# Layer 1's experts over fifteen sorted tiles of 128 tokens

## The reference

```
def _moe(x, Wg, W1, b1, W2, b2):          # 1024 tokens, E = 8, D = 128, DF = 512
    xf = x.reshape(S * B, D)
    idx = jnp.argmax(xf @ Wg.T, axis=-1)
    out = jnp.zeros_like(xf)
    for e in range(E):
        m = (idx == e)[:, None].astype(xf.dtype)
        h = jax.nn.relu(xf @ W1[e] + b1[e])
        out = out + m * (h @ W2[e] + b2[e])
    return out.reshape(S, B, D)
y = _layer_norm(x + _mha(...), g1, be1)
z = _layer_norm(y + _moe(y, Wg, W1, b1, W2, b2), g2, be2)
```

## Time and profile before

| what | us |
|---|---|
| median of 3 runs | 1155.62 |
| lowest and highest of them | 1153.92, 1157.77 |
| span of the profiled execution | 1150.6 |
| its time outside the span | not listed; the median lies 5.0 above the span |
| TensorE busy (matmuls) | 949.3 (83%) |
| VectorE busy | 581.6 (51%) |
| ScalarE busy | 439.1 (38%) |
| GpSimd busy | 223.4 (19%) |

### The profile page before, as it was taken

The page is one execution under the profiler, slowest core; times in us unless marked ns, Lnnn a source line. Parts: engine busy times, 40 slices in busy tenths (PEclk is TensorE's granted clock), DMA queues, the critical chain, the costliest instruction groups (busy, mean ns, idle before and its releaser), DMA issues. The chain is left out here.

```text
span 1150.6 us, 15643 instructions
## 1 busy us (share of the span) xinstructions
PE 949.3 (83%) x5673; PEld 649.8 (56%) x5673; DVE 581.6 (51%) x1264; ACT 439.1 (38%) x769; POOL 223.4 (19%) x258
## 2 busy tenths in 40 slices
PE   6885799759947459999777968998699988879998
PEld 4673345349935236777537832233366676747776
DVE  4885446265377553111765857775264448631111
ACT  2341445433323013334352414776332233333443
POOL 0552301000053030000373534001000013320110
PEclk9995979869969759999997976999899989978999
DMA  7004410215410000110000051400001010000111
GB/s 305 1 33 106 127 31 23 111 73 160 138 33 0 1 0 19 38 37 19 1 1 1 2 133 36 116 22 2 0 29 41 27 38 1 1 1 19 37 37 37
DMA packets 30159, 52.72 MB, mean 46 GB/s; under 512 B 3152, under 2 KB 22800, under 8 KB 29712
## 3 DMA queue, kind: packets, MB, share of 16 engines
q1 hardware_dynamic: 29584, 50.83, 14.7%
q0 software_dynamic: 512, 1.05, 0.4%
HBM read 43.81 MB, written 7.86 MB: 45 GB/s over the span
## 5 line engine op out<-in xcount | busy, mean ns | idle before, releaser
L2334 PE MATMUL psum<-xT_all,wexp 128*128 128x512 f32 x400 | 184.9, 607 | 1.2 <-issue 0.7
L1502 DVE TENSOR_REDUCE arena<-psum 128x2 f32<-128x1024 f32 (+3 forms) x128 | 127.1, 1020 | 78.8 <-PE psum L2111 49.1
L1031 ACT ACTIVATE arena<-psum 128x512 f32<-128x512 f32 (+3 forms) x256 | 115.9, 516 | 85.1 <-PE psum L2124 47.4
L2334 PEld LDWEIGHTS psum<-xT_all,wexp 128*128 128x128 f32 x400 | 74.6, 196 | 78.9 <-issue 73.9
L732 POOL TENSOR_TENSOR rstd<-var,held 128x8 f32<-128x8 f32 (+3 forms) x22 | 46.1, 2116 | 375.1 <-DVE var L1257 362.2
L2349 PEld LDWEIGHTS psum<-wexp,arena 128*128 128x128 f32 x800 | 95.9, 195 | 15.0 <-issue 14.8
L2108 PE MATMUL psum<-arena 72*128 72x512 bf16 (+3 forms) x256 | 82.7, 395 | 25.1 <-DMA arena<-parts_q 12.3
L2036 PE MATMUL psum<-values_out_all,arena 128*128 128x128 f32 x560 | 77.0, 285 | 26.7 <-ACT arena L995 26.7
L2349 PE MATMUL psum<-wexp,arena 128*128 128x128 f32 x800 | 96.2, 278 | 0.0
L807 POOL TENSOR_TENSOR arena<-arena,small 128x616 f32<-128x616 f32 x56 | 67.9, 1215 | 124.9 <-DVE small L1434 124.6
L1781 DVE SCALAR_TENSOR_TENSOR x_res<-psum,arena,x_res 128x128 f32<-128x128 f32 x136 | 38.4, 344 | 101.9 <-PE psum L2349 101.7
(11 more groups left out here) (289 smaller groups left out, 1488.1 us busy)
## 6 DMA issues: line engine op xcount, KB each, us to landing
wexp<-experts SPq DMA_DIRECT2D x24, 514.0 KB, 3.7
parts_k<-wexp SPq DMA_DIRECT2D x12, 384.0 KB, 2.9
arena<-parts_k SPq DMA_DIRECT2D x48, 96.0 KB
arena<-parts_q SPq DMA_DIRECT2D x48, 96.0 KB
arena<-experts SPq DMA_DIRECT2D x8, 514.0 KB, 3.6
arena<-rows SPq DMA_DIRECT2D x8, 512.0 KB, 8.1
wexp<-experts SPq DMA_DIRECT2D x9, 384.0 KB, 3.2
held<-packed SPq DMA_DIRECT2D x1, 2375.0 KB, 15.6
```

The costliest lines, as they stand in the source:

```text
L1031: act.activation(p_self[:, n % 2, kt % 2, j, lo:S], bank(t_bank("keys", c, k), lo, S), ACT.Exp, scale=DS ** -0.5).then_inc(ut_ok, 1)
L1502: dve.tensor_reduce(top[:, x % 2, qt, j:j + 2], src, AX_X, ALU.max, negate=True).then_inc(us_ok, 1)
L2334: mm(bank(c, 0, BANK), wexp[:, side, c * P:(c + 1) * P], xT_all[:, b * S:(b + 1) * S], start=True, stop=True).then_inc(h_ps, 1)
```

## The change

Layer 1's experts no longer run over all tokens. DVE (`places1`) finds each token's expert, counts the tokens of each expert, rounds each count up to whole tiles of 128, and gives each token a row in a queue of 15 tiles (8 tiles of tokens and at most 7 more by rounding) and each tile its expert. POOL scatters the 8 token tiles of r_res with 8 indirect DMAs into the DRAM tensor `queued`, which SP has cleared in layer 0. SP reads the tile's expert into a register (`value_load`), loads that expert's weights into one of the four buffers W0 and the queue's tile into `xin`. PE turns the tile, makes 4 hidden and 4 output matmuls of 128x128; ACT rectifies; DVE copies out; SP stores to `answers`; POOL gathers 8 tiles by the same places; DVE adds them to r_res. `add_biases` waits until the scatter has read r_res, and `centre_weights` stands between the places and that wait. `prep(2)` on PE now waits for the last copy out and the biases. Constants of 152 columns are added to the packed weights, and the semaphore counts of layers 2 and 3 (KB, HB, WB) are lowered.

```diff
+TILES1 = B * S // P + 8 - 1
...
@@ SP, layer 0, after the loads of rows
+            sp.dma_start(queued, zeros).then_inc(cleared, 16)
...
-            for l in range(1, 4):
+            def queues1():
+
+                def weights(j):
+                    e = sp.value_load(tile_e[0:1, j:j + 1], min_val=0, max_val=7)
+                    src = experts[1].rearrange("e p n -> p e n")[:, bass.ds(e, 1), :]
+                    sp.dma_start(W0[j % 4].unsqueeze(1), src).then_inc(w0_in[j % 4], 16)
+
+                def tokens(j):
+                    sp.dma_start(D["xin"][:, j % 4 * P:(j % 4 + 1) * P], queued[j * P:(j + 1) * P, :]).then_inc(q_in[j % 4], 16)
+
+                sp.wait_ge(tiles_ok, 1)
+                for j in range(4):
+                    weights(j)
+                sp.wait_ge(sent, 16 * NT)
+                for j in range(4):
+                    tokens(j)
+                for j in range(TILES1):
+                    if j + 4 < TILES1:
+                        sp.wait_ge(d_T, AFTER0 + j + 1)
+                        tokens(j + 4)
+                        sp.wait_ge(d_O, AFTER0 + j + 1)
+                        weights(j + 4)
+                    sp.wait_ge(d_y, HELD0 + j + 1)
+                    sp.dma_start(answers[j * P:(j + 1) * P, :], D["y"][:, j % 4 * P:(j % 4 + 1) * P]).then_inc(d_stored[j % 4], 16)
+
+            queues1()
+            for l in range(2, 4):
...
@@ POOL, after inverse_norms
+                pool.wait_ge(cleared, 16)
+                pool.wait_ge(m_xn, 2 + B)
+                pool.wait_ge(slots_ok, 2)
+                for t in range(NT):
+                    pool.indirect_dma_start(queued, bass.IndirectOffsetOnAxis(ap=slot_i[:, t:t + 1], axis=0),
+                                            r_res[:, t * P:(t + 1) * P], None).then_inc(sent, 16)
+                for side in range(4):
+                    pool.wait_ge(d_stored[side], STORED0 + 16 * len(range(side, TILES1, 4)))
+                for t in range(NT):
+                    pool.indirect_dma_start(D["back"][:, t * P:(t + 1) * P], None, answers,
+                                            bass.IndirectOffsetOnAxis(ap=slot_i[:, t:t + 1], axis=0)).then_inc(d_back[t // TB], 16)
...
@@ ACT
+            def experts1():
+
+                turned_gates(1)
+                for j in range(TILES1):
+                    act.wait_ge(w0_in[j % 4], 16 * (E0 // 4 + j // 4 + 1))
+                    if j >= 2:
+                        act.wait_ge(d_O, AFTER0 + j - 1)
+                    act.wait_ge(d_H, AFTER0 + j + 1)
+                    for c in range(4):
+                        last = act.activation(D["h"][:, j % 2 * BANK + c * P:j % 2 * BANK + (c + 1) * P],
+                                              bank(2 + j % 2, c * P, (c + 1) * P), ACT.Relu,
+                                              bias=W0[j % 4][:, 1024 + c:1025 + c])
+                    last.then_inc(d_h, 1)
...
@@ DVE, places1
+                top_mask(m, t3(logits), 0, shape)
+                step.then(dve.memset(pre[:, 0, :], 0.0))
+                for t in range(1, NT):
+                    step.then(dve.tensor_tensor(pre[:, t, :], pre[:, t - 1, :], m[:, t - 1, :], ALU.add))
+                dve.tensor_tensor(M["tot"][:, 0:E_], pre[:, NT - 1, :], m[:, NT - 1, :], ALU.add).then_inc(g_m, 1)
+                dve.tensor_copy(gates[:, :, 0:E_], m).then_inc(gate_ok, 1)
+                dve.wait_ge(g_loc, 2)
...
+                dve.tensor_scalar(slot_i[:, 0:NT], small[:, 0, 48:56], 1.0, None, ALU.subtract).then_inc(slots_ok, 1)
...
+                dve.tensor_scalar(tile_e[:, 0:16], small[:, 1, 40:56], 7.0, None, ALU.min).then_inc(tiles_ok, 1)
@@ DVE
+            def experts1():
+
+                def features(j):
+                    dve.wait_ge(d_T, AFTER0 + j + 1)
+                    if j >= 2:
+                        dve.wait_ge(d_H, AFTER0 + j - 1)
+                    dve.tensor_copy(D["xe"][:, j % 2 * P:(j % 2 + 1) * P], bank(j % 2, 0, P)).then_inc(d_xe, 1)
+
+                def answer(j):
+                    dve.wait_ge(d_O, AFTER0 + j + 1)
+                    if j >= 4:
+                        dve.wait_ge(d_stored[j % 4], STORED0 + 16 * (j // 4))
+                    dve.tensor_copy(D["y"][:, j % 4 * P:(j % 4 + 1) * P], bank(4 + j % 2, 0, P)).then_inc(d_y, 1)
+
+                places1()
+                centre_weights()
+                dve.wait_ge(sent, 16 * NT)
+                add_biases(1)
+                features(0)
+                features(1)
+                for j in range(TILES1):
+                    if j + 2 < TILES1:
+                        features(j + 2)
+                    answer(j)
+                for b in range(B):
+                    r_ = r_res[:, b * S:(b + 1) * S]
+                    dve.wait_ge(d_back[b], BACK0 + 16 * TB)
+                    step.then(dve.tensor_tensor(r_, r_, D["back"][:, b * S:(b + 1) * S], ALU.add))
...
@@ PE
+            def places1():
+                n = NT * 8
+                pe.wait_ge(g_m, 2)
+                mm(bank(0, n, n + 8), w("ones"), M["tot"][:, 0:8], start=True, stop=True)
+                mm(bank(0, 0, n), w("before"), M["m12"][:, 0:n], start=True, stop=True)
+                mm(bank(0, 0, n), w("ones"), M["pre"][:, 0:n], start=False, stop=True, skip_group_check=True).then_inc(g_loc, 1)
...
+                places1()
+                turned_gates(1)
+                biases(1)
+                pe.wait_ge(slots_ok, 2)
+                turned(0)
+                turned(1)
+                hidden(0)
+                for j in range(TILES1):
+                    if j + 2 < TILES1:
+                        turned(j + 2)
+                    if j + 1 < TILES1:
+                        hidden(j + 1)
+                    output(j)
```

More of the change, by code:

```diff
@@ L80, in constants, with queue_constants @@
         "queue": np.broadcast_to(np.arange(E0, dtype=f) * CAPACITY - 1, (P, E0)),
+    }
+def queue_constants():
+    e = np.arange(8)
+    wide = lambda v: np.broadcast_to(np.asarray(v, np.float32).reshape(1, -1), (P, np.size(v)))
+    return {
+        "r_steps": wide(P * e),
+        "r_ahead": wide(P * (e[None, :] < e[:, None])),
+        "r_within": wide(e[None, :] <= e[:, None]),
+        "r_tile": wide(np.arange(16)),
     }
@@ L164, in row_layout, with program @@
     return np.concatenate([w1.reshape(8, 4, P, P).transpose(0, 2, 1, 3).reshape(8, P, 4 * P), w2], 2)
-def program(nc, x, mask, packed, experts, rows, out, answers, parts_q, parts_k, at):
+def program(nc, x, mask, packed, experts, rows, zeros, out, answers, queued, parts_q, parts_k, at):
     ctx = ExitStack()
@@ L313, in program @@
         f_stat, f_rstd, f_done = sems("f_stat f_rstd f_done")
+        cleared, tiles_ok, sent = sems("cleared tiles_ok sent")
+        q_in = [sem(f"q_in{n}") for n in range(4)]
         t1_e, t1_p, t1_av = sems("t1_e t1_p t1_av")
@@ L1208, in _ @@
                     selfattn(l // 2)
-                if l:
-                    experts(l)
-                else:
+                if l == 0:
                     gating(l)
                     experts0()
+                elif l == 1:
+                    experts1()
+                else:
+                    experts(l)
         @block.vector
@@ L1759, in experts @@
             def experts(l):
-                acc = r_res if l == 1 else x_res
+                acc = x_res
                 gflat = M["gates"]
@@ L2438 @@
     answers = nc.dram_tensor("answers", (SLOTS, P), F32, kind="Internal").ap()
+    queued = nc.dram_tensor("queued", (TILES1 * P, P), F32, kind="Internal").ap()
     parts_q = nc.dram_tensor("parts_q", (2, B, 3 * P, S), BF16, kind="Internal").ap()
     parts_k = nc.dram_tensor("parts_k", (2, B, 3, 3 * P, S), BF16, kind="Internal").ap()
-    program(nc, ap["x"], ap["mask"], ap["packed"], [ap[f"experts{l}"] for l in range(4)], ap["rows"], out, answers,
-            parts_q, parts_k, at)
+    program(nc, ap["x"], ap["mask"], ap["packed"], [ap[f"experts{l}"] for l in range(4)], ap["rows"], ap["zeros"], out, answers,
+            queued, parts_q, parts_k, at)
     r = run_bass_kernel_spmd(nc, [arrays], core_ids=[0])
```

73 lines of the change are left out of this document (62 added, 11 removed).

## The result

| | us |
|---|---|
| before, median of 4 runs on the same chip | 1156.69 (1153.92 to 1159.71) |
| after, median of 4 runs | 1108.46 (1105.86 to 1109.69) |
| ratio | 0.9587, 95% interval 0.9563 to 0.9611 |
| predicted | 1109.0, range 1098 to 1130 |

What follows compares the result with a forecast made beforehand. The prediction took TensorE to bound layer 1's experts. Its terms summed to 75.0 us instead of 121.8, a span of 1103.8; adding 5.0 outside the span gave 1109, range 1098 to 1130.

Steps and rivals of the forecast that it cites:

- Places: After the logits' copy, finding each token's expert, counting and assigning queue rows: 6.8 us, bounds 6 to 8.
- Scatter: POOL's eight scatters into the queue, until VectorE goes on: 11.8 us, bounds 11 to 14, sized from layer 0's gather.
- Tokens back: After the scatter, SP's issue of a 64 KB token load and its landing: 2.4 us in all.
- First tile: First expert tile, with TensorE starting at the low clock after idling: 6.4 us.
- Fourteen more tiles: The tiles after the first, paced by the DMA engines' rate: 2.3 us each, bounds 1.9 to 3.0, 32.2 in all.
- The weights' ring: In the tiles, each weight load waits for an earlier output; three tiles take 5.75 us plus SP's expert read: 2.2 each.
- v: In the tiles, SP's read of the expert number from SBUF into a register: 0.8 us, between 0.029 and 1.5.
- What follows: After the tiles, layer 2's earlier preparation (up to -2.3 us) against its queries at the low clock (up to +4): taken as 0.
- Outside the span: Added to the predicted span: 5.0 us, by which the median of three earlier runs lay above the profiled execution's span.
- A: Rival: the low clock holds through the tiles, 3.8 us each, 21 us more, 1130 us; chance 0.10.
- B: Rival: SP paces the tiles at 2.8 to 3.8 us each, giving 1116 to 1130 us; chance 0.14.
- C: Rival: the weight loads' round trip makes the kernel slower; at 18 us a tile takes 6.7, 1170 in all; chance 0.05.

Runs made afterwards that it cites:

- the kernels of the table: The changed kernel, its repeat and eight variants with one or several further edits, compared stretch by stretch from the logits' copy to the closing norm's statistics.
- warm kernel: Fifteen unread 128x512 matmuls added on TensorE to the changed kernel, before the first tile and layer 2's cross-attention: 1105.99 us, ratio 0.9556.
- six buffers and tokens ahead: Against the changed kernel: six expert-weight buffers in place of four, and all fifteen token tiles loaded before the first tile: 1100.73 us, ratio 0.952.
- the kernel with tokens ahead: Against the changed kernel: fifteen token buffers in place of four, all asked for before the first tile: 1104.52 us, ratio 0.9553.
- the two kernels with one edit each: Against the changed kernel: one loads all token tiles before the first tile (ratio 0.9553), the other has six weight buffers in place of four (0.961).

## Why the prediction was right, step by step

The forecast case came true, and the time too (1109.0, the profiled execution 1109.69), but partly by terms that cancel: the stretch 2.4 longer than the sum, what lies ahead of the logits' copy 1.6 longer, and 3.2 less outside the span. 1109.0 + 2.4 + 1.6 - 3.2 = 1109.8. That it agrees to within 1 us is luck: the end of the logits' copy alone moves by 4.5 us among the kernels of the table.

- *Places*, 6.8: measured 6.62.
- *Scatter*, 11.8: from the slots at 436.12 to VectorE at 448.59 it is 12.5. Layer 0's gather was a fair measure: eight issues 1.34 apart (1.264 there) and landing 2.3 after the last began. New is POOL's start, 0.84 after the slots. VectorE's centring lay beside it (437.27 to 442.8). Three of the five issues up to there took 1.07 to 1.17 in place of 0.96, 0.5 us together; whether the centring is the cause was not tested.
- *Tokens back*, 2.4: 450.43 - 448.59 = 1.84.
- *First tile*, 6.4: 5.61. The low clock was there, as the forecast had it: window 448.60 to 456.00 at 0.59, and 1.14 us of it went away in the warm kernel. The clock rose just ahead of the first output (0.66 from 454 to 455, 1.00 from there to 456), earlier than the forecast had it.
- *Fourteen tiles*, 32.2 at 2.3: 34.21 at 2.44, inside the bounds 1.9 to 3.0. The right size came from a wrong reason. I had taken the largest of three, the DMA engines' rate of 283 GB/s in proportion to their share. That is no ceiling: in the kernel after they moved 405 GB/s at full share while the first weights came in,

```profile
444.00:446.00 2.00, 0.00 (x0) 0.00 (x0) 0.00 (x0) 0.00 (x0) 1.70 (x2) 0.50 1.02 405
```

and with six buffers and tokens ahead they moved 325 GB/s in the middle of the tiles, at 1.90 a tile. The weights' ring, put at 2.2, was the step that was right in kind and short in one size: the landing, 4.6 in place of 3.7. It is 4.6 with the tokens' loads beside it and without them, and no run takes apart what stretches it. With SP's read and what lies before the issue at 0.7 (v and the 0.15 of the forecast, 0.95 there) it gives (0.7 + 4.6 + 0.11 + 0.89 + 0.89) / 3 = 2.40, the 2.39 of the kernel with tokens ahead. What the forecast missed is the second ring, the tokens': SP asks for tile 11's rows only after it has issued tile 10's weights and tile 6's store. One turn of it in the kernel after, with the answers of tiles 6 and 9 at its ends:

```profile
471.32 0.29 DVE L1841 COPY arena<-psum 128x128 f32<-128x128 f32 x1 [1.50 <-PE psum L2469]
...
472.01 0.34 SPq L720 DMA_DIRECT2D arena<-experts  x1
...
472.39 1.06 SPq L738 DMA_DIRECT2D answers<-arena  x1
...
473.50 0.43 SPq L723 DMA_DIRECT2D arena<-queued  x1
...
477.13 0.33 PE L2452 MATMUL psum<-held,arena 128*128 128x128 f32 x1 [0.62 <-DMA arena<-queued]
...
479.29 0.29 DVE L1841 COPY arena<-psum 128x128 f32<-128x128 f32 x1 [1.50 <-PE psum L2469]
```

  From copy to copy, 0.69 to the weights' issue, 0.38 to the store's, 1.11 to the tokens' (0.48 in most turns), 3.63 to the turn and 2.16 to the answer: 7.97 for three tiles, 2.66; with 0.48 it is 7.34, 2.45. The ring was argued from these rows; that it is a limit of its own is shown by the two kernels with one edit each. What makes it so long is the landing of the 64 KB loads (L723). The first four, with nothing else in flight, landed in 1.7 to 2.0; those of the tiles have this line:

```profile
DMA to landing us min/median/max: 3.1/3.9/4.7
```

  With 1.9 in place of 3.9 the ring would be 1.8 a tile, an estimate from these rows, and no limit beside TensorE's 1.9. The two sums of 2.40 and 2.45 lie near the table's means and under the pace of the middle tiles, 2.60 with tokens ahead and 2.79 in the kernel after; where the other 0.2 to 0.3 of a middle tile goes is open.
- *v*, 0.8: from an output's last copy to the weights' issue it is 0.7. The floor of some 600 ns that the Trainium skill's "DMA: Bandwidth & Descriptors", section "Latency and other measured facts", gives for a tensor load does not stand here: the rows of L718 have 276 ns, and 0.45 with the register work that follows. Its price in time, with the expert fixed: 1.2 to 2.3 us.
- *Store* 2.9 and *gather* 11.8: 4.40 and 11.5. The store is the term that moves most from one execution to the next (2.7 to 4.8).
- *What follows*, 0: right in both parts. From the norm's statistics to the first queries it took 24.59 before and 22.04 after, 2.5 less (the 2.32 of ACT's squares is in it); against it the queries ran cold, 7.50 us for twelve passes in place of 5.40. The first of these rows is of the kernel before, the second of that after:

```profile
574.23 5.40 PE L1979 MATMUL psum<-held,xT_all 128*128 128x512 f32 x12 [2.91 <-DVE keys_of_tokens L1323]
```

```profile
528.94 7.50 PE L2118 MATMUL psum<-held,xT_all 128*128 128x512 f32 x12 [2.08 <-DVE keys_of_tokens L1399]
```

  To the end it is 601.0 after and 600.96 before; so close an agreement is luck, since 599.5 to 606.3 stand for the same code in the kernels of the table.
- *Outside the span*, 5.0: mis-sized. I had set the median of the runs against the span of another execution. Each run listed with its span, before or after, has 1.8 to 2.0 (1109.69 and 1107.9; before, 1157.09 and 1155.3), so the profiled execution of before took about 1152.4, below the three runs that were given.

The rivals: the low clock held only up to the first tile, 0.50 to 0.59, and was 1.00 in the tiles (A fell). The Trainium skill's page "TensorE: Matmul & The Clock Gate", section "Why this matters for your kernels", warns of a long wait for a DMA between matmuls; the prediction left out the word "long". Here the waits of 0.2 to 1.1 us for rows did not bring the clock down. SP did not pace the tiles (B): it idled between its three issues, but its order stood in the tokens' ring. The weights' round trip (C) was real, at a third of its feared size: 4.6 + 0.7 in place of 14.8.

## What to carry to other kernels

Where each step asks for its next loads behind its own output, count the ring for every kind of load, and for each the number of tiles that it spans, not that of its buffers: here both had three, since TensorE's order put the load's first reader ahead of an earlier tile's output. When a limit goes away and the time stays, look at the waits again before giving up; two rings hid from either edit alone a gain of 0.5 us a tile. And a first tile behind a long wait on DMA runs at the low clock; unread matmuls until the data land gave it back where they ended 0.47 us before, and did not where they ended 1.65 before.

## What was not expected of the hardware

The DMA share is no measure of the rate left: 277 GB/s stood at 1.01 in the tiles of the kernel after (460 to 464), 325 at 0.95 in those with tokens ahead and six buffers, and 405 at 1.02 with weight loads and scatters alone. An indirect scatter by POOL is as cheap to issue as a gather (0.96 us busy, up to 1.17 in three of eight issues) and lands in 2.2 to 4.7 us; the gathers landed in 2.4 to 2.6. A 64 KB load of rows landed in 1.7 to 2.0 us by itself and in 3.1 to 4.7 beside weight loads and stores.
